# A two-layer perceiver kernel: half of each cross-attention step's scores kept with keys on partitions, and softmax division moved behind the values

## The reference, cut to what matters

```python
xn = layernorm(x)
q, k, v = xn @ Wq + bq, ctx @ Wk + bk, ctx @ Wv + bv        # 16 heads of 16
logits = q @ k.T * 16**-0.5 (+ mask * -1e9 in layer 0)       # 64 queries, 1024 keys, per head
x = x + (softmax(logits) @ v) @ Wo + bo
```

## Time and profile before

| | us |
|---|---|
| median of 3 runs (lowest, highest) | 1368.8 (1368.15, 1373.0) |
| the profiled execution's own time | 1374.19 |
| its span, first to last instruction | 1371.8 |
| TensorE busy | 1273.0 (93%) |
| VectorE, ScalarE, GpSimd busy | 925.9, 801.7, 744.5 |

### The profile page before, as it was taken

The page is one execution under the profiler, slowest core; times in us unless marked ns, Lnnn a source line. Parts: engine busy times, 40 slices in busy tenths (PEclk is TensorE's granted clock), DMA queues, the critical chain, the costliest instruction groups (busy, mean ns, idle before and its releaser), DMA issues. The chain is left out here.

```text
span 1371.8 us, 28654 instructions
## 1 busy us (share of the span) xinstructions
PE 1273.0 (93%) x11120; PEld 884.1 (64%) x11122; DVE 925.9 (67%) x1799; ACT 801.7 (58%) x1373; POOL 744.5 (54%) x497
## 2 busy tenths in 40 slices
PE   6999999999999999897978999999899999998886
PEld 3666666666667675555646667666666666676654
DVE  4786686776666664674768766677766769765674
ACT  3766666666666664543655665666576655665331
POOL 1865656556665652330016676566656667856633
PEclk9999999999999999998999999999999999999998
DMA  4322112111122103002640031001010222000000
GB/s 157 85 86 64 52 47 68 47 48 48 47 85 77 49 9 108 1 1 65 215 125 32 32 93 54 32 16 49 32 53 32 63 63 63 32 1 1 5 9 20
DMA packets 30533, 74.24 MB, mean 54 GB/s; under 512 B 4032, under 2 KB 16192, under 8 KB 26176
## 3 DMA queue, kind: packets, MB, share of 16 engines
q1 hardware_dynamic: 30400, 72.41, 17.3%
HBM read 65.06 MB, written 7.34 MB: 53 GB/s over the span
## 5 line engine op out<-in xcount | busy, mean ns | idle before, releaser
L655 POOL TENSOR_TENSOR ca_prob<-ca_prob,ca_inv_sum 128x1024 f32<-128x1024 f32 x256 | 493.2, 1935 | 349.9 <-DVE ca_inv_sum L892 348.9
L732 PEld LDWEIGHTS bank<-ident,ca_prob 128*128 128x128 f32 x2048 | 238.3, 142 | 77.6 <-issue 54.8
L732 PE MATMUL bank<-ident,ca_prob 128*128 128x128 f32 x2048 | 268.4, 275 | 7.7 <-DVE ca_v L841 4.6
L856 DVE CUSTOM_DVE_ANT_0 ca_neg_logit<-bank,ca_mask_add 128x1024 f32<-128x1024 f32 x128 | 151.6, 1222 | 103.8 <-PE bank L722 76.6
L859 DVE TENSOR_REDUCE ca_neg_max<-bank 128x1 f32<-128x1024 f32 x128 | 150.6, 1218 | 72.3 <-PE bank L722 72.2
L802 ACT ACTIVATE ca_prob<-bank,ca_neg_max 128x1024 f32<-128x1024 f32 x128 | 142.5, 1114 | 79.9 <-DVE ca_neg_max L859 79.8
L802 ACT ACTIVATE ca_prob<-ca_neg_logit,ca_neg_max 128x1024 f32<-128x1024 f32 x128 | 146.9, 1149 | 68.4 <-DVE ca_neg_max L856 68.3
L869 DVE COPY ca_probT<-bank 128x512 f32<-128x512 f32 x256 | 163.8, 682 | 15.7 <-PE bank L732 15.7
L813 ACT ACTIVATE ca_probT<-bank 128x512 f32<-128x512 f32 x256 | 139.5, 594 | 44.3 <-PE bank L732 41.8
L722 PE MATMUL bank<-ca_kT,ca_q_blk 32*128 32x512 f32 x1024 | 147.3, 645 | 4.6 <-DVE ca_v L841 2.7
L772 ACT ACTIVATE ca_kT<-bank,ca_bk 64x512 f32<-64x512 f32 x128 | 87.4, 683 | 104.7 <-PE bank L667 103.8
(11 more groups left out here) (302 smaller groups left out, 1699.0 us busy)
## 6 DMA issues: line engine op xcount, KB each, us to landing
ca_ctxT<-in_ctxT SPq DMA_DIRECT2D x16, 1024.0 KB, 5.3
ctxT<-in_ctxT SPq DMA_DIRECT2D x16, 1024.0 KB, 4.8
ca_mask_i<-in_mask SPq DMA_DIRECT2D x32, 256.0 KB, 6.2
ek_ctxT<-in_ctxT SPq DMA_DIRECT2D x12, 512.0 KB, 5.6
early_k<-ek_out SPq DMA_DIRECT2D x48, 128.0 KB, 3.4
ca_kT<-early_k SPq DMA_DIRECT2D x12, 512.0 KB, 5.7
lat<-in_x SPq DMA_DIRECT2D x1, 1024.0 KB, 4.7
out<-lat SPq DMA_DIRECT2D x8, 128.0 KB, 1.9
```

The source lines that it names most:

```text
L655: pool.tensor_tensor(self.prob[:, x, :], self.prob[:, x, :], self.inv_sum[:, x:x + 1].broadcast_to([P, CTX]), ALU.mult).then_inc(self.norm ...
L732: tr = pe.transpose(self.core.bank[:, x, n * P:(n + 1) * P], self.prob[:, 2 * (s % 2) + p, (4 * h + n) * P:(4 * h + n + 1) * P], self.core ...
L856: dve.tensor_tensor_reduce(self.neg_logit[:, p, :], scores, self.mask_add[:, b % 2, :], -1.0, BIG, ALU.add, ALU.min, self.neg_max[:, y:y + ...
```

## The change

Of a step's four heads, the two in rows 32 to 63 and 96 to 127 of the array (the "row" heads) stay as they were. The other two (the "column" heads) are computed with the operands swapped, so that keys lie on partitions and the result is already what `probT` needs.

- `scores`: two 128x512 products for the row heads into banks 2 and 3, and eight 128x128 products for the column heads into banks 0 and 1.
- For the column heads the keys of a query lie across partitions and in eight chunks, so their maximum is found in stages: `column_maxima` takes, per query, the maximum over the eight key chunks; `turn_column_max` transposes it on TensorE; `tops` (VectorE) reduces it to one number per query; `spread_top` spreads it over all partitions by a transpose on TensorE; `below_tops` subtracts it from the scores into `probT`; `column_exponentials` (ScalarE) exponentiates in place.
- The division leaves `normalise` and goes behind the values: GpSimd adds the eight chunks of the column heads (`add_columns`) and spreads the row sums (`spread_rows`); `times_v` adds six small products that put each head's sum beside its weighted values; `take_pv` takes the reciprocal of 128x64 and multiplies; GpSimd joins the heads and adds the value bias (`join_heads`), which `take_v` no longer adds.
- `transposes` has one pair instead of two, and ScalarE takes both of its banks. The value and key projections are split in two parts, with the two small transposes between them. The weighted values of steps s-2 and s-1 now stand at the end of an even step.
- The mask is loaded a second time with keys on partitions (`mask_keys`, `mask_col`). Banks 5 to 7 rotate, bank 4 serves the two small transposes.
- The loops of second_layer are changed in the same way; without a mask, `column_maxima` and `below_tops` read the scores in their banks. The diff below leaves them out, with the buffers, semaphores and loads.

```diff
-    def __init__(self, core, sem, rotating=range(4, 8)):
+    def __init__(self, core, sem, rotating=range(5, 8)):
...
     def convert_mask(self, pool, b):
...
+        pool.tensor_scalar(self.mask_col[:, b % 2, :, :], self.mask_col_i[:, :, :], NEG, None, ALU.mult)\
+            .then_inc(self.mask_ready, 1)
         pool.tensor_scalar(self.mask_add[:, b % 2, :], self.mask_i[:, :], NEG, None, ALU.mult).then_inc(self.mask_ready, 1)
...
-    def normalise(self, pool, s):
-        for p in range(2):
-            x = 2 * (s % 2) + p
-            pool.wait_ge(self.inv_ready, 2 * s + p + 1)
-            pool.tensor_tensor(self.prob[:, x, :], self.prob[:, x, :], self.inv_sum[:, x:x + 1].broadcast_to([P, CTX]),
-                               ALU.mult).then_inc(self.norm_ready, 1)
...
+    def add_columns(self, pool, s):
...
+        pool.wait_ge(self.column_exp, s + 1)
+        wait(pool, self.column_sum_ready, s)
+        p, f = self.columns(s), self.fold
+        pool.tensor_tensor(f[:, :, :], p[:, 0:4, :], p[:, 4:8, :], ALU.add).then_inc(self.fold_step, 1)
+        pool.wait_ge(self.fold_step, 2 * s + 1)
+        pool.tensor_tensor(f[:, 0:2, :], f[:, 0:2, :], f[:, 2:4, :], ALU.add).then_inc(self.fold_step, 1)
+        pool.wait_ge(self.fold_step, 2 * s + 2)
+        if n >= 2:
+            self.banks.wait_filled(pool, ("pv", n - 2))
+        pool.tensor_tensor(self.column_sum[:, s % SUMS, :], f[:, 0, :], f[:, 1, :], ALU.add)\
+            .then_inc(self.column_sum_ready, 1)
...
+    def spread_rows(self, pool, s):
...
+        pool.wait_ge(self.exp_done, s + 1)
+        if n >= 2:
+            self.banks.wait_filled(pool, ("pv", n - 2))
+        pool.tensor_tensor(self.spread_sum[:, s % SUMS, :], self.core.half_pick,
+                           self.row_sum[:, s % 2:s % 2 + 1].broadcast_to([P, 2 * HD]), ALU.mult)\
+            .then_inc(self.row_sum_ready, 1)
...
+    def join_heads(self, pool, n):
...
+        pool.wait_ge(self.picked_ready, n + 1)
+        self.banks.wait_taken(pool, ("pv", n))
+        if b >= 4:
+            self.banks.wait_filled(pool, ("o", b // 2 - 2))
+        attn = self.attnT[:, m, b % 4 * S:(b % 4 + 1) * S]
+        pool.tensor_tensor(attn, self.picked[0][:, n % 2, :], self.picked[1][:, n % 2, :], ALU.add)\
+            .then_inc(self.attn_step, 1)
+        pool.wait_ge(self.attn_step, 2 * n + 1)
+        pool.tensor_tensor(attn, attn, self.bv[:, m:m + 1].broadcast_to([P, S]), ALU.add).then_inc(self.attn_step, 1)
...
-            pe.wait_ge(self.max_ready if self.masked else self.exp_done, 2 * s)
+            if self.masked:
+                pe.wait_ge(self.masked_ready, s)
+                pe.wait_ge(self.max_ready, s)
+            else:
+                pe.wait_ge(self.below_ready, s)
+                pe.wait_ge(self.exp_done, s)
         for half in range(2):
-            for j in range(2):
-                rows = slice(S * half + 32 * j, S * half + 32 * j + 32)
-                mm = pe.matmul(self.core.bank[:, 2 * j + half, :], self.q_blk[rows, b % 2, u, :, :],
-                               self.kT[rows, b % 2, u, :], start=True, stop=True, tile_position=(S * half + 32 * j, 0))
-        mm.then_inc(self.scores_ready, 1)
...
+            rows = slice(S * half + 32, S * half + 64)
+            mm = pe.matmul(self.core.bank[:, 2 + half, :], self.q_blk[rows, b % 2, u, :, :], self.kT[rows, b % 2, u, :],
+                           start=True, stop=True, tile_position=(S * half + 32, 0))
+        mm.then_inc(self.row_scores, 1)
+        for c in range(4):
+            for half in range(2):
+                rows = slice(S * half, S * half + 32)
+                mm = pe.matmul(self.core.bank[:, half, c * P:(c + 1) * P], self.kT[rows, b % 2, u, c * P:(c + 1) * P],
+                               self.q_blk[rows, b % 2, u, :, :], start=True, stop=True, tile_position=(S * half, 0))
+        mm.then_inc(self.col_scores, 1)
+    def turn_column_max(self, pe, s):
+        pe.wait_ge(self.column_max_ready, s + 1)
+        x = self.banks.open(pe, ("turned", s), 4)
+        self.banks.done(pe.transpose(self.core.bank[:, x, 0:P], self.column_max[:, s % 2, :], self.core.ident[:, :]),
+                        ("turned", s))
+    def spread_top(self, pe, s):
+        self.banks.wait_taken(pe, ("turned", s))
+        x = self.banks.open(pe, ("spread", s), 4)
+        self.banks.done(pe.transpose(self.core.bank[:, x, 0:P], self.top[:, s % 2:s % 2 + 1].broadcast_to([P, P]),
+                                     self.core.ident[:, :]), ("spread", s))
+    def transposes(self, pe, s):
+        pe.wait_ge(self.exp_done, s + 1)
...
-        for s in (2 * n, 2 * n + 1):
-            for p in range(2):
-                for h in range(2):
-                    self.banks.wait_taken(pe, ("t", s, p, h))
+        for s in self.step_of_values(n):
+            for h in range(2):
+                self.banks.wait_taken(pe, ("t", s, h))
         for i in range(4):
             self.banks.wait_taken(pe, ("v", 4 * b + i))
+        pe.wait_ge(self.column_exp, 2 * n + 2)
...
+        pe.wait_ge(self.column_sum_ready, 2 * n + 2)
+        pe.wait_ge(self.row_sum_ready, 2 * n + 2)
+        for e in range(2):
+            for s in self.step_of_values(n):
+                j = 2 * (s % 2)
+                pe.matmul(self.core.bank[32 * j:32 * j + 32, x, P:P + S], self.core.head_ones[:, e, :],
+                          self.column_sum[:, s % SUMS, e * S:(e + 1) * S], start=(e == 0), stop=(e == 1),
+                          tile_position=(0, 32 * j))
+        for s in self.step_of_values(n):
+            j = 2 * (s % 2) + 1
+            mm = pe.matmul(self.core.bank[32 * j:32 * j + 32, x, P:P + S], self.spread_sum[:, s % SUMS, :],
+                           self.core.two_ident, start=True, stop=True, tile_position=(0, 32 * j))
         self.banks.done(mm, ("pv", n))
...
     def exponentials(self, act, s):
...
+        y = s % 2
+        act.wait_ge(self.max_ready, s + 1)
...
+        source = self.neg_logit[:, :] if self.masked else self.core.bank[:, 2:4, :].rearrange("p a n -> p (a n)")
+        act.activation(self.prob[:, y, :], source, ACT.Exp, bias=self.neg_max[:, y:y + 1],
+                       scale=-1.0 if self.masked else 1.0, accum_out=self.row_sum[:, y:y + 1]).then_inc(self.exp_done, 1)
+    def column_exponentials(self, act, s):
+        if self.masked:
+            self.banks.wait_taken(act, ("spread", s))
+        else:
+            act.wait_ge(self.below_ready, s + 1)
+        act.activation(self.columns(s), self.columns(s), ACT.Exp).then_inc(self.column_exp, 1)
...
+    def column_maxima(self, dve, s):
...
+        dve.wait_ge(self.col_scores, s + 1)
...
+        scores = self.core.bank[:, 0:2, :].rearrange("p a (c q) -> p (a c) q", q=P)
+        if self.masked:
+            if s % GROUPS == 0:
+                dve.wait_ge(self.mask_ready, 2 * b + 2)
+            if s >= 1:
+                self.banks.wait_taken(dve, ("spread", s - 1))
+            dve.tensor_tensor(self.masked_col[:, :, :].rearrange("p c (e q) -> p c e q", q=S),
+                              scores.rearrange("p c (e q) -> p c e q", q=S),
+                              self.mask_col[:, b % 2, :, :].unsqueeze(2).broadcast_to([P, NCH, 2, S]), ALU.add)\
+                .then_inc(self.masked_ready, 1)
+            dve.wait_ge(self.masked_ready, s + 1)
+            scores = self.masked_col[:, :, :]
+        dve.tensor_reduce(self.column_max[:, y, :], scores.rearrange("p c q -> p q c"), AX.X, ALU.max)\
+            .then_inc(self.column_max_ready, 1)
...
+    def row_maxima(self, dve, s):
...
+        scores = self.core.bank[:, 2:4, :].rearrange("p a n -> p (a n)")
+        wait(dve, self.exp_done, s if self.masked else s - 1)
+        if self.masked:
+            dve.tensor_tensor_reduce(self.neg_logit[:, :], scores, self.mask_add[:, b % 2, :], -1.0, BIG,
+                                     ALU.add, ALU.min, self.neg_max[:, y:y + 1]).then_inc(self.max_ready, 1)
+        else:
+            dve.tensor_reduce(self.neg_max[:, y:y + 1], scores, AX.X, ALU.max, negate=True).then_inc(self.max_ready, 1)
...
+    def tops(self, dve, s):
...
+        x = self.banks.wait_filled(dve, ("turned", s))
+        self.banks.free(dve.tensor_reduce(self.top[:, s % 2:s % 2 + 1], self.core.bank[:, x, 0:P], AX.X, ALU.max),
+                        ("turned", s))
...
+    def below_tops(self, dve, s):
...
+        x = self.banks.wait_filled(dve, ("spread", s))
+        tops, shape = self.core.bank[:, x, 0:P], [P, NCH, P]
+        if self.masked:
+            self.banks.free(dve.tensor_tensor(self.columns(s), self.masked_col[:, :, :],
+                                              tops.unsqueeze(1).broadcast_to(shape), ALU.subtract), ("spread", s))
+        else:
+            self.banks.free(dve.tensor_copy(self.tops_row[:, :], tops), ("spread", s))
+            self.banks.wait_taken(dve, ("spread", s))
```

(36 more changed lines are left out.)

274 lines of the change are left out of this document (140 added, 134 removed).

## The result

| | before | after |
|---|---|---|
| median us (lowest, highest) | 1370.9 (1368.15, 1373.93) | 1462.8 (1462.37, 1465.3) |
| ratio, 95% interval | | 1.067 (1.064 to 1.070) |
| the profiled execution's time, its span | 1374.19, 1371.8 | 1465.3, 1462.1 |
| steps 0 to 62 of the first layer | 473.18 | 567.65 |
| step 63 and the stages between the layers | 223.11 | 220.98 |

The change made the kernel 6.7% slower. Nearly all of it lies in the first layer, the one with the mask: +94.5 us. The second layer came out 1 us shorter.

What follows compares the result with a forecast made beforehand. TensorE was taken as the bound. First layer +40, second layer +8 and tail +3 gave +51 us: the profiled 1374.2 becomes 1425, the median 1368.8 becomes 1420, range 1378 to 1490.

Steps and rivals of the forecast that it cites:

- main case: Whole kernel: slower as summed, by the first layer's new wait, spanning 1385 to 1455 us; chance 0.62.
- rival 3: Column maximum on VectorE reads slowly, up to twice 1.22 us, in both layers: 1543 us; chance 0.10.
- second layer +8: Second layer: no wait for the column maximum, steps sum to -14, bank waits +22; ends -17 and +35.
- no-wait pair: An odd and an even step on TensorE without waits: 5.81 plus 7.98, 13.79 us, 1.0 less than now.
- sums: TensorE's six added products of 64 columns per pair of steps: 0.28 us, bounds 0 and 1.3.
- The wait before turn_column_max: First layer, each step: TensorE idles 0.88 us for VectorE's mask addition and maximum, +0.99 with a weight load; bounds 0.7 and 1.2.
- Rival 2: Scores in both layers: column products wait for the row products' second pass, +0.43 us in 128 steps, +55, 1475; chance 0.14.
- The covers: First layer: spread_top's wait lies behind TensorE's work; GpSimd's additions, about 1.0, 0.55 and 0.3 us, are hidden too.
- The last three steps: End of the first layer, steps without keys: less work to cover the wait with, +4 us.
- int8 steps: First layer's eight-bit weight preparation on VectorE: about 0.5 us of room in odd steps instead of 2, three weights, +7.
- The floor: Second layer: column scores held until below_tops, so a step cannot be shorter than about 6.7 us, 6.5 without keys.
- +22 for bank waits: Second layer: three banks rotate instead of four, a bank waited for about 1 us, 22 times; bounds 0 and 40.

Runs made afterwards that it cites:

- e1_neighbours: The changed kernel with the first layer's column maximum taken over 8 neighbouring values instead of 8 lying 128 apart, column mask -10 instead of -1e9: 1412.8 us (1.030).

## Why the forecast was right or wrong

Forecast 1420, measured 1463: the direction and the wait behind it held, the size was 43 us short, and 1463 lies above the 1385 to 1455 that I gave the main case alone. By my own sign ("Column maxima of 1.2 us, else rival 3") the case that came was rival 3 in the first layer. By stage, forecast against the change of the spans: first layer +40 and +94.5; second layer +8 and -1.1; the rest +3 and -3.1 (start +0.8, between the layers -2.1, tail -1.7).

- **TensorE's work.** Right. The no-wait pair was forecast as 13.79 and is 13.80. Its parts: scores 1.07, measured 1.10; sums 0.28, measured 0.33 (387.88 to 388.21).
- **The wait before turn_column_max.** Right in place, releaser and frequency, wrong in size: 0.88 us idle forecast, 1.50 measured. The step that failed is "VectorE takes the maximum over it ... 1220 ns for a maximum over 1024 values in memory". That row read neighbours; the new one reads 16 bytes or more apart and takes 1930. With 1220 the wait was 0.81 to 0.86 and the first layer +44.0, against +40 forecast: this one term is 50 of the 54 us missing there (43 of idle time, 7 of TensorE's busy time, at a granted clock of 0.98 against 0.99 for the layer). The bounds that I put on the wait (0.7 to 1.2) left this out of the sum, although rival 3 named it.
- **Rival 3, the slow read.** Right in kind for the first layer. I priced it at twice 1.22 (it is 1.6 times) and let it hold for the banks as well: there, 128 apart, the maximum takes 1.22. So its 1543 came out 80 too high, and the chance of 0.10 too low for something that a rule spoke for and no row against.
- **Rival 2, scores one after the other.** Not so in the order that the change has: column products, written behind the row products, start 0.01 us after them (388.21, 388.22) and run beside their first passes. With the order turned round the scores take 0.52 us longer and the kernel 48.5 us, near the +0.43 a step and +55 I gave that case. So the Trainium skill's sentence ("TensorE: Matmul & The Clock Gate", The mechanism) that matmuls stay in program order was not the limit I took it for: by it, as I read it, scores would have been 1.5 us or more, and they took 1.10. The order of writing matters, but here a product on another row tile did not wait for the second pass of one written ahead of it.
- **The covers.** spread_top was covered, as forecast, but only because the first wait stood ahead of it: with that gone TensorE idled there (25.5 us in 59 places, 0.43 each). GpSimd's smaller sums were hidden but dearer than my proportional estimate: 1.28, 0.73 and 0.47 us for 512, 256 and 128 values, not 1.0, 0.55 and 0.3.
- **The first layer's ends.** Step 0 grew by 7.4 us, which I had not costed: VectorE waits for GpSimd's two mask conversions, and the granted clock is 0.72 on average over the step, where it was 1.00 before. The last three steps cost +10.1 (26.99 against 16.90) where I had +4; 6.7 of that with the fast maximum. int8 steps were forecast at +7; they were not tested singly.
- **The second layer.** +8 forecast, -1 measured, from two errors against each other. The floor is 6.92 us, not 6.7: TensorE idles 26.1 us in 20 steps for below_tops. And I had missed that TensorE waited 15.7 us for GpSimd before. In sum, TensorE's busy time in the layer fell by 22.6 us (486.79 to 464.21) and its idle time rose by 21.5 (29.6 to 51.1); half of what it is now idle is that one wait for below_tops. How much of the +22 for bank waits came true is open.

Where the first-layer maximum was given its forecast length (e1_neighbours), the first layer's sum was off by 4 us in 40. The plain pair (15.74 against 15.77) comes from the forecast's mechanism, with two small misses that cancel: VectorE started 0.23 us after the scores instead of 0.13, and TensorE's transpose came 0.05 after the maximum instead of 0.12. The small remainder of the layer is luck: step 0 cost 6.4 us that the sum didn't have and the last three steps 2.7 more than it had, against 5.1 less in the steps between. The range of 1378 to 1490 held because of rival 2's price, not because the maximum's length was inside it.

## What to carry to other kernels

A chain of two operations on another engine inside TensorE's step costs what it is longer than the cover; find the piece that needn't be in it. Here the mask addition need not precede a maximum that is only a bound, as long as the bound is not too far above the unmasked scores, and with the top moved up the change turns from 6.7% slower into 1.4% faster. For a reduction, look at the distance of the innermost values and at where they lie, not at their count: in memory 16 and 512 bytes apart cost 1.6 times, 512 bytes apart in a bank nothing. A wait can also cost more than its idle time, where the granted clock is lower in the same steps.

## What the hardware showed that was not expected

- VectorE's maximum over 128 groups of 8 float32: 1220 ns at 4 and 8 bytes apart in memory, 1973 at 16, 1931 at 512; 1225 from the banks at 512.
- VectorE with both operands in memory and GpSimd's sums took turns: 1.37 us for an operation on 256 values whose shortest was 0.42, 1.68 for one of 1.27.
- Eight short products behind two long ones, in other row tiles: 1.10 us for both. In front of them: 1.62.
